# Score maxima of an attention layer: 36 full PSUM banks a unit in place of 48 part-filled ones, and one masked maximum over the whole width of each diagonal piece

## The reference, cut to what matters

```
xn = layernorm(x)                                   # (4, 1024, 128)
q, k, v = split(xn @ w_qkv)                         # 16 heads, 8 channels each
wei = softmax(where(causal, q @ k.T * 8**-0.5, -inf))
x = x + (wei @ v) @ w_proj + b_proj
      + sum over the 2 best experts of gate * (gelu(xn @ W1 + b1) @ W2 + b2)
```

## Time and profile before

| | |
|---|---|
| median of the runs | 850.88 us |
| the profiled execution | 850.34 us |
| its span in the trace | 848.6 us |
| TensorE matmul busy | 724.0 us (85%) |
| VectorE busy | 550.9 us (65%) |
| ScalarE busy | 450.2 us (53%) |
| GpSimd busy | 301.7 us (36%) |
| mean granted TensorE clock | 0.904 of 2.4 GHz |

### The profile page before, as it was taken

One profiled execution on the slowest core, in us unless ns is written; L12 is line 12 of the kernel. 1 busy time (PEld: TensorE's weight loads), 2 busy tenths in 40 slices (PEclk: granted clock), 3 DMA queues, 4 the chain that ended last, 5 costly groups with the idle time before them and its releaser, 6 DMA issues.

```text
span 848.6 us, 15145 instructions
## 1 busy us (share of the span) xinstructions
PE 724.0 (85%) x5018; PEld 413.0 (49%) x5018; DVE 550.9 (65%) x2138; ACT 450.2 (53%) x715; POOL 301.7 (36%) x477
## 2 busy tenths in 40 slices
PE   0889889887887798788989899788999898998985
PEld 0745445443443545455555455445555456565433
DVE  5666676765555476667676666667666667667656
ACT  0224734414334467566576657566666657566543
POOL 6532620466775033342324122332314122323401
PEclk9966975968887699999999889999989999899988
DMA  9452850211315807044443507044433517030262
GB/s 234 98 121 86 184 142 4 54 44 44 91 48 145 259 22 214 13 116 121 108 117 93 146 22 210 13 114 124 128 97 92 147 37 219 16 104 17 77 167 74
DMA packets 95652, 88.34 MB, mean 104 GB/s; under 512 B 8528, under 2 KB 83064, under 8 KB 95576
## 3 DMA queue, kind: packets, MB, share of 16 engines
q1 hardware_dynamic: 90680, 77.27, 33.9%
q0 software_dynamic: 4544, 9.35, 3.4%
q10 hardware_dynamic: 352, 0.78, 0.4%
HBM read 50.18 MB, written 21.32 MB: 84 GB/s over the span
## 4 chain that ended last, share of the span: by engine, by line
PE 66%; DVE 21%; issue 5%; ACT 4%; DMA 1%; another core or an unknown queue 1%; POOL 0%; ACTq 0%; SPq 0%; DVEq 0%; POOLq 0%
PE aux L836 16%; PE ov L868 16%; PE aux L926 10%; PE aux L878 7%; DVE maxes L1060 5%; DVE maxes L1064 4%; PE sc L790 3%; PE sc L791 2%; PE sc L792 2%; DVE junk L1065 2%; ACT probs L743 2%; DVE xrow L1116 2%; PE sc L854 2%; PE aux L883 1%; PE aux L906 1%
## 5 line engine op out<-in xcount | busy, mean ns | idle before, releaser
L743 ACT ACTIVATE probs<-sc 128x1024 f32<-128x1024 f32 (+3 forms) x384 | 296.3, 811 | 232.1 <-PE sc L854 208.3
L836 PE MATMUL aux<-kT,qT 32*128 32x512 f32 (+3 forms) x768 | 226.4, 462 | 70.5 <-DVE maxes L1060 17.5
L652 POOL TENSOR_SCALAR_AFFINE_SELECT probs<-probs 128x256 f32<-128x256 f32 x256 | 104.6, 415 | 383.0 <-ACT probs L743 379.3
L1060 DVE TENSOR_REDUCE maxes<-aux 128x1 f32<-128x512 f32 x256 | 163.4, 684 | 57.0 <-PE aux L836 51.4
L836 PEld LDWEIGHTS aux<-kT,qT 32*128 32x128 f32 x768 | 102.6, 195 | 189.9 <-DVE maxes L1060 41.8
L1064 DVE TENSOR_REDUCE maxes<-aux 128x1 f32<-128x128 f32 (+2 forms) x384 | 161.2, 420 | 46.1 <-PE aux L836 40.9
L868 PE MATMUL ov<-probs,v 128*32 128x512 f32 (+3 forms) x1536 | 181.2, 546 | 0.7 <-POOL probs L652 0.2
L854 PE MATMUL sc<-qT,kT 32*128 32x512 f32 (+3 forms) x768 | 163.0, 446 | 7.5 <-DMA qT<-mT 3.0
L1065 DVE CUSTOM_DVE_ANT_0 junk<-aux,cst 128x128 f32<-128x128 f32 x512 | 139.1, 282 | 18.5 <-PE aux L836 18.4
L677 POOL DMA_INDIRECT ys<-ysb,back x78 | 75.9, 973 | 82.3 <-DVE ysb L1103 39.4
L878 PE MATMUL aux<-wh 128*128 128x384 f32 x339 | 92.4, 401 | 9.5 <-DVE maxes L1060 6.9
(11 more groups left out here) (119 smaller groups left out, 626.7 us busy)
## 6 DMA issues: line engine op xcount, KB each, us to landing
w1b<-w_scr SPq DMA_DIRECT2D x39, 512.0 KB, 4.4
w2all<-in_L_ffn_W SPq DMA_DIRECT2D x39, 256.0 KB
xs<-ysb SPq DMA_DIRECT2D x13, 387.0 KB, 7.0
xrow<-in_L_attn_x SPq DMA_DIRECT2D x8, 512.0 KB, 6.6
kT<-kqh SPq DMA_DIRECT2D x32, 128.0 KB, 2.8
w_scr<-w1b SPq DMA_DIRECT2D x8, 512.0 KB, 5.0
qT<-kqh SPq DMA_DIRECT2D x30, 128.0 KB, 2.7
xsin<-xs SPq DMA_DIRECT2D x6, 516.0 KB
```

Of the source, the lines that this page charges most:

```text
L652: nc.gpsimd.affine_select(out=block_, in_=block_, compare_op=ALU.is_ge, fill=0.0, base=0, pattern=[[0, 2], [1, P]], channel_multiplier=-1) ...
L743: nc.scalar.activation(probs[:, s % 2, 2 * half:2 * half + 2, 0:cols], pair(part)[:, :, 0:cols], ACT.Exp).then_inc(sc_done, 1)
L836: nc.tensor.matmul(bank(part)[:, 0:cols], qT[n % 3][rows, P * i:P * i + P], kT[n % 3][rows, k0:k0 + cols], start=True, stop=True).then_inc ...
L1060: nc.vector.reduce_max(maxes[:, i, slot, h:h + 1], bank(part)[:, 0:cols], axis=AX.X).then_inc(aux_d, 1)
```

## The change

- `MAXES` becomes a list of banks. Each bank holds one or two pieces of the same head, side by side, 512 columns in all: (tile 0, 128) with (tile 2, 384); (tile 3, 512); (tile 1, 256) with the diagonal piece of tile 5 (256); the four full pieces of tiles 4 to 7; the diagonal pieces of tile 4 (128) with tile 6 (384); that of tile 7 (512). A head has 9 banks, a unit 36. The 12 products of a head stay as they are; where a bank has two, only the second signals VectorE.
- Each diagonal piece is taken by one fused add-the-mask-and-take-the-maximum over its whole width. The mask is 512 wide, zero but in its last 128 columns. `junk` is gone: the elementwise result is written back over the piece in PSUM. `maxes` has 2 slots a tile in place of 3.
- The deal of the maxima follows the new count: 18 before unit 0 for 24; 3 beside each `hidden` block (3 or 4 blocks) for 12 over all; the rest of the 36 over the 12 steps, 2 a step or 9 in 4 steps, for 3 a step; about 3 a step for 4 in the other units. The credit of a bank in `array_use` is 128 columns.
- The constants grow by 384 columns; `zero` is a part of the mask in place of a tile of its own (one memset less); `stats` moves into a free part of another tile.

```diff
-MAXES = [(i, 0, P * (i + 1), True, 0) for i in range(4)] + \
-        [x for i in range(4, TPB) for x in ((i, 0, W, False, 1), (i, W, P * (i + 1) - W, True, 0))]
+MAXES = [[(0, 0, P, 0), (2, 0, 3 * P, 0)], [(3, 0, W, 0)], [(1, 0, 2 * P, 0), (5, W, 2 * P, 0)]] + \
+        [[(i, 0, W, 1)] for i in range(4, TPB)] + [[(4, W, P, 0), (6, W, 3 * P, 0)], [(7, W, W, 0)]]
 NM = HG * len(MAXES)
-HALF_M = HG * 4
-EARLY_M = 24
+HALF_M = HG * 3
+EARLY_M = 18
...
+BESIDE_M = 3
...
     if n in GROUP_OF:
-        return [3] * NS
-    first = {0: [8, 8, 8], 1: [6, 5, 5], 2: [8, 8, 8]}.get(n, [6, 5, 5])
-    rest = {0: 32, 1: 24, UNITS - 1: 0}.get(n, 32)
+        rest = NM - BESIDE_M * len(blocks_of(GROUP_OF[n]))
+        return [rest * (i + 1) // NS - rest * i // NS for i in range(NS)]
+    first = {0: [6, 6, 6], 2: [6, 6, 6]}.get(n, [4, 4, 4])
+    rest = {0: 24, 1: 18, UNITS - 1: 0}.get(n, 24)
...
-            parts.extend(take(12 // len(blocks_of(f))))
+            parts.extend(take(BESIDE_M))
...
-        return MAXES[part[2] // HG][2] // 4
+        return W // 4
...
# TensorE, part "max"
-                    nc.tensor.matmul(bank(part)[:, 0:cols], qT[n % 3][rows, P * i:P * i + P],
-                                     kT[n % 3][rows, k0:k0 + cols], start=True, stop=True).then_inc(aux_ready, 1)
+                    for i, k0, cols, _ in MAXES[s]:
+                        last_ = nc.tensor.matmul(bank(part)[:, at:at + cols], qT[n % 3][rows, P * i:P * i + P],
+                                                 kT[n % 3][rows, k0:k0 + cols], start=True, stop=True)
+                        at += cols
+                    last_.then_inc(aux_ready, 1)
...
# VectorE, part "max"
-                    if not diagonal:
-                        nc.vector.reduce_max(maxes[:, i, slot, h:h + 1], bank(part)[:, 0:cols], axis=AX.X).then_inc(aux_d, 1)
-                    else:
-                        if cols > P:
-                            other = 1 if i < 4 else 2
-                            nc.vector.reduce_max(maxes[:, i, other, h:h + 1], bank(part)[:, 0:cols - P], axis=AX.X)
-                        nc.vector.tensor_tensor_reduce(out=junk[:, AUXI[part] % 3, :], in0=bank(part)[:, cols - P:cols],
-                                                       in1=cmask, scale=1.0, scalar=LOW, op0=ALU.add, op1=ALU.max,
-                                                       accum_out=maxes[:, i, 0, h:h + 1]).then_inc(aux_d, 1)
+                    for i, _, cols, slot in MAXES[s]:
+                        dst, src = maxes[:, i, slot, h:h + 1], bank(part)[:, at:at + cols]
+                        if slot:
+                            last_ = nc.vector.reduce_max(dst, src, axis=AX.X)
+                        else:
+                            last_ = nc.vector.tensor_tensor_reduce(out=src, in0=src,
+                                                                   in1=cmask[:, W - cols:W], scale=1.0, scalar=LOW,
+                                                                   op0=ALU.add, op1=ALU.max, accum_out=dst)
+                        at += cols
+                    last_.then_inc(aux_d, 1)
```

More of the change, by code:

```diff
@@ L42 @@
 VPAD = 32
-K_ID, K_MASK, K_U, K_ONE = 0, P, 2 * P, 3 * P
-K_RANK = 4 * P
+K_ID, K_MASK, K_U, K_ONE = 0, P, P + W, 2 * P + W
+K_RANK = 3 * P + W
 K_THR = K_RANK + E
@@ L377, in layer_kernel @@
         cst = sb("cst", [P, CONSTS])
-        ident, cmask = cst[:, K_ID:K_ID + P], cst[:, K_MASK:K_MASK + P]
+        ident, cmask = cst[:, K_ID:K_ID + P], cst[:, K_MASK:K_MASK + W]
         upper, ones = cst[:, K_U:K_U + P], cst[:, K_ONE:K_ONE + P]
@@ L394, in layer_kernel @@
         xh, xl = sb("xh", [P, TOK], F32R), sb("xl", [P, TOK], F32R)
-        stats = sb("stats", [P, NT, 6])
         meanvar, rstd, veps, half_ = sb("meanvar", [P, NT, 2]), sb("rstd", [P, NT]), sb("veps", [P, NT]), sb("half", [P, E])
@@ L400, in layer_kernel @@
         qT = [sb(f"qT{i}", [P, T], F32R) for i in range(3)]
-        zero = sb("zero", [P, C])
+        zero = cmask[:, 0:C]
         v = sb("v", [P, NT * H * VD + VPAD])
         probs = sb("probs", [P, 2, HG, W])
-        maxes, mrow = sb("maxes", [P, TPB, 3, HG]), sb("mrow", [P, 4, HG])
+        maxes, mrow = sb("maxes", [P, TPB, 2, HG]), sb("mrow", [P, 4, HG])
         mneg, mT = sb("mneg", [P, HG, D, 4]), sb("mT", [P, P])
-        junk = sb("junk", [P, 3, P])
         ot, rden = sb("ot", [P, 2, W]), sb("rden", [P, 4, HG])
@@ L429, in gtile @@
             return tmp[:, i * NT * E:(i + 1) * NT * E].rearrange("p (t e) -> p t e", e=E)
+        stats = tmp[:, 6 * NT * E:6 * NT * E + NT * 6].rearrange("p (t s) -> p t s", s=6)
         logits, eq, first1, rest, first2, slotv = (gtile(i) for i in range(6))
@@ L504, in _ @@
                     if n < 3:
-                        sp.wait_ge(zeroed, 9)
+                        sp.wait_ge(zeroed, 8)
                     else:
@@ L594, in _ @@
             nc.gpsimd.memset(zrow[:, :, 0:C], 0.0)
-            nc.gpsimd.memset(zero[:, :], 0.0).then_inc(zeroed, 1)
             for i in range(3):
@@ L689, in _ @@
                 if part == ("relay", 0):
-                    act.wait_ge(zeroed, 9)
+                    act.wait_ge(zeroed, 8)
                     act.wait_ge(aux_d, D_AFTER["qk", 0, 1, 1])
@@ L831, in _ @@
                     s, h = divmod(m, HG)
-                    i, k0, cols, _, _ = MAXES[s]
-                    rows = slice(32 * h, 32 * h + 32)
+                    rows, at = slice(32 * h, 32 * h + 32), 0
                     if m == 0:
                         pe.wait_ge(relayed[n % 3], relays(n))
-                    nc.tensor.matmul(bank(part)[:, 0:cols], qT[n % 3][rows, P * i:P * i + P],
-                                     kT[n % 3][rows, k0:k0 + cols], start=True, stop=True).then_inc(aux_ready, 1)
+                    for i, k0, cols, _ in MAXES[s]:
[3 more added lines that the diff above has]
+                    last_.then_inc(aux_ready, 1)
                 elif what == "rows":
@@ L1056, in _ @@
                     s, h = divmod(m, HG)
-                    i, _, cols, diagonal, slot = MAXES[s]
+                    at = 0
                     dve.wait_ge(aux_ready, AUXI[part] + 1)
-                    if not diagonal:
-                        nc.vector.reduce_max(maxes[:, i, slot, h:h + 1], bank(part)[:, 0:cols], axis=AX.X).then_inc(aux_d, 1)
-                    else:
-                        if cols > P:
-                            other = 1 if i < 4 else 2
-                            nc.vector.reduce_max(maxes[:, i, other, h:h + 1], bank(part)[:, 0:cols - P], axis=AX.X)
-                        nc.vector.tensor_tensor_reduce(out=junk[:, AUXI[part] % 3, :], in0=bank(part)[:, cols - P:cols],
-                                                       in1=cmask, scale=1.0, scalar=LOW, op0=ALU.add, op1=ALU.max,
-                                                       accum_out=maxes[:, i, 0, h:h + 1]).then_inc(aux_d, 1)
+                    for i, _, cols, slot in MAXES[s]:
[8 more added lines that the diff above has]
+                    last_.then_inc(aux_d, 1)
                 elif what == "negate":
@@ L1129, in shape_constants @@
     c[:, K_ID:K_ID + P] = np.eye(P)
-    c[:, K_MASK:K_MASK + P] = np.triu(np.full((P, P), MASKED), 1)
+    c[:, K_MASK + W - P:K_MASK + W] = np.triu(np.full((P, P), MASKED), 1)
     c[:, K_U:K_U + P] = np.triu(np.ones((P, P)), 1)
```

## The result

The changed kernel takes 795.14 us (median of 4 runs, 791.83 to 800.04), the kernel before 849.56 us beside it. The ratio is 0.934, with a 95% interval of 0.925 to 0.943. The profiled execution took 800.04 us with a span of 798.3; against 848.6 that is 50.3 us less.

A forecast was written before the change was run, and what follows sets the result against it. TensorE was taken to bound the kernel (busy 85%, 66% of the chain), with VectorE's maxima holding up its banks. 850.3 - 32.3 + 3.6 - 5.6 + 0 + 9.0 - 2.9 + 0.6 = 822.7, so 823 us; forecast range 798 to 836.

The forecast's parts named there:

- step 1: Maxima on the three banks: fewer banks go round, half of 64.6 us of TensorE waits gone, -32.3 us (bounds 0, 64.6).
- The reason given for 798: Clock ahead of the experts: 75 us at half clock worth at most 34 us, half of that sets the low end.
- The named waits: TensorE's matmuls idle before maxima products, mostly for VectorE: 64.6 us, forecast to fall to about half.
- the kql wait: Third maximum waits 0.96 us for the k and q split; forecast gone there, but `down` late in 12 steps, +3.6 us.
- Step 2: VectorE's maxima: 384 fewer instructions save 27 us of VectorE, -5.6 us on the path (bounds 0, 27).
- step 3: Masked maximum's write-back into PSUM: taken as 0; other bound a second pass, 170 us of VectorE.
- the half-rate rival: Write-back into PSUM at half rate: VectorE gets 170 us more, kernel slower at 874 us; chance 0.10.
- Step 4: TensorE, 192 banks with two products of one head on the same 32 rows: +9.0 us (bounds 0, 37).
- Step 5: The rest: 323 fill products for 339, -2.9 us; constants grow by 197 KB, +0.6 us.
- the waits move on: Scores and values wait for ScalarE in place of the bank, fewer banks bring nothing: 855 us; chance 0.14.

The follow-up runs named there:

- e1: Kernel before with its 48 banks and deal, only the masked maximum taken over a diagonal piece's whole width, result written back into PSUM: ratio 0.999 (0.995 to 1.004).

## Why the prediction was right in its way and wrong in its size

**The way and its cause held, the size did not.** The forecast was 823 us, 3.2% less, and the range ended at 798. That end lies above the bound that step 1 itself gave: with all 64.6 us gone, the sum is 790. The reason given for 798, half of 34 us, leads from 823 only to 806. By its steps:

*Step 1, fewer banks go round: this is the term that was mis-sized.* The named waits fell by 34 us, as it said, and the kql wait left the maxima and came back at `down` with 1.4 us for the 3.6 named. But I took TensorE's idle rows for the whole price of the third maximum. Much of that price stands in rows that count as busy, of which 29 us went: a row of 512 columns lasts 0.49 us, where streaming them takes about 0.24 (an estimate, twice the 0.12 us for 256 columns of the earlier trace rows), so that a product held back by up to some 0.25 us shows no wait. Measured as phases, each third maximum cost 0.44 us, 44 us over 100 steps of the expert units alone; 33 of them are left net, since the change has phases of 0.92 and 1.69 us too. Half of 64.6 was the wrong thing to halve; the length of the phase in the trace of before, with the 0.33 us between the halves of the scores where nothing stands between them, would have shown it.

*Step 2, VectorE's instructions:* the count was right, the -5.6 us was not. e1 measures 0 for this and step 3 together.

*Step 3, the write-back:* there is no second pass, 512 columns take 720 ns and not 1,200, and the half-rate rival is out. But its price is not 0: 512 x 0.05 = 26 us of VectorE, 27 saved. "Perfetto Trace Analysis" of the Trainium skill, section "Optimizing Scalar/DVE Operations", gives VectorE about 60 ns of access overhead on SBUF and 125 on PSUM, a difference of 65 by estimate. It was the better guide than the nearest rows: the accumulator read grew by 59 ns and the instruction of 128 columns by 34, with 50 ns back to back.

*Step 4, two products of one head in a row:* 9.0 us is neither borne out nor refuted. Two pairs of TensorE after, beside the `hidden` blocks:

```profile
540.58 0.33 PE L837 MATMUL aux<-kT,qT 32*128 32x128 f32 x2
```

```profile
540.74 0.39 PE L837 MATMUL aux<-kT,qT 32*128 32x384 f32 x2
```

These are two heads side by side: within a pair the second product starts 0.16 us behind the first, 0.11 more than the 0.05 that the forecast took for streaming 128 columns, where it had 0.12 and 0.07. What that costs depends on what stands beside it. Beside `scores` of 512 columns, 13 of 20 phases with two pairs of 256 columns take 0.67 or 0.68 us, as with two single products; what lifts the mean to 0.92 is above all five phases of 1.5 to 1.9 us with waits for banks, and five with three banks. Beside four `hidden` blocks, 12 banks with 16 products in place of 12 take 7.9 us for 7.5, 0.1 for each second product. Over 192 pairs that is, by estimate, 0 to some 20 us; no run takes the pairs away alone. "TensorE: Matmul & The Clock Gate" of the Trainium skill, Part 3, has a weight load overlap running products only where the row group differs. For the start of the second 32-row product the trace agrees in direction, at 0.11 us of the 0.18 to 0.20 of a whole load; the full-array rows that I set against it were no evidence for this shape.

*Step 5:* 323 fills, as counted. The load of the constants grew from 354.5 to 546.5 KB and lands after 4.8 us for 4.5.

The 50.3 us of the two profiles lie here: 33.0 in the phases of the expert units, 11.5 in the stretches beside `hidden`, less 3.0 given back in the rest of these units, 9.9 ahead of them, and 1.1 given back behind. The first is step 1, fewer third maxima, with what the pairs cost in it. Beside `hidden` the gain is in the units with three blocks, where 9 banks stand in place of 12 (5.4 us for 7.6). What the 9.9 us ahead are made of is not shown. **Of the rivals**, "the waits move on" happened in part, by some 22 us in all; two thirds of it are one wait: TensorE now stands 14.8 us for GpSimd's masks behind its scatters in the units ahead of the experts, where it stood 0.2:

```profile
PE ov L871 <- POOL probs L653: 14.8, 6, 6.5
```

**Open** is what a second product of one head costs by itself, and how much of VectorE's time lies on the path: 50 us more on full pieces cost about 5 us and 19 us less on diagonal ones gave 9 to 14, with intervals of 6 to 11 us to either side of each ratio.

## What to carry to other kernels

On a ring of few banks served in order, ask for each product which part filled its bank last. Here the third maximum of a step needed the bank of the part just ahead, and cost 0.44 us on average in the crowd, with 128 or 512 columns and however fast VectorE reduced the maxima, while two maxima beside the scores fit into 0.67 us. So fewer parts a step than banks is worth more than faster emptying. Size such a change from the length of the phase in the trace and what it would be without the part, not from the idle time: here 22 us of idle time went, and 50 us of the kernel. When a result of VectorE is thrown away, throw it into SBUF.

## What was not expected of the hardware

- The accumulator read behind a masked maximum takes 142 ns where the elementwise result goes to PSUM and 83 ns where it goes to SBUF, with the same destination of the maximum itself.
- Two 32-row products of one head start 0.16 us apart with 128 columns in the first; two heads' pairs run side by side all the same, and beside the scores two such pairs of 256 columns fit into the phase of two single products.
- Cutting all products for maxima to 128 columns made nothing faster (0.968 for 0.953, 0.907 for 0.893), with less clock granted in the profiles.
